# Self-attention and the masked cross-attention behind it in one block of a two-layer decoder kernel

## The reference

```python
x = _layernorm(x + _L0_attn_ref(x, ...))                  # gated recurrence
x = _layernorm(x + _L0_xattn_ref(x, ctx, ctx, mask, side, ...))
x = _layernorm(x + _L0_ffn_ref(x, ...))
x = _layernorm(x + _L1_attn_ref(x, ...))                  # self-attention, relative positions
x = _layernorm(x + _L1_xattn_ref(ctx, ctx, x, mask, ...)) # masked cross-attention
x = _layernorm(x + _L1_ffn_ref(x, ...))                   # gated feed-forward

# _L1_xattn_ref
k = (key @ Wk.T + bk); v = (value @ Wv.T + bv); q = (query @ Wq.T + bq)   # 16 heads each
scores = jnp.where(mask, q . k, -1e10)
out = softmax(scores / 4) . v
return out @ Wo.T + bo
```

## Time and profile before

| | us |
|---|---|
| median of 3 runs | 926.36 |
| lowest and highest | 924.04, 928.03 |
| profiled execution, its own time | 927.1 |
| its span in the trace | 925.3 |
| TensorE busy | 861.7 (93%) |
| VectorE busy | 681.9 (74%) |
| ScalarE busy | 620.9 (67%) |
| GpSimd busy | 413.0 (45%) |
| first and second barrier | at 298.0 and 627.7 |

### The profile page before, as it was taken

One profiled execution on the slowest core, in us unless ns is written; L12 is line 12 of the kernel. 1 busy time (PEld: TensorE's weight loads), 2 busy tenths in 40 slices (PEclk: granted clock), 3 DMA queues, 4 the chain that ended last, 5 costly groups with the idle time before them and its releaser, 6 DMA issues. The chain is left out here.

```text
span 925.3 us, 21117 instructions
## 1 busy us (share of the span) xinstructions
PE 861.7 (93%) x7006; PEld 621.4 (67%) x7017; DVE 681.9 (74%) x2515; ACT 620.9 (67%) x1608; POOL 413.0 (45%) x428
## 2 busy tenths in 40 slices
PE   9998989999987788999999999897999999999996
PEld 7876766777666466777777776675666666655554
DVE  4988888888877656687686676525888878866875
ACT  4548677777762367787787787735888888864441
POOL 2256246567342345434444342243455555326432
PEclk9999999999998899999999999997999999999998
DMA  9334100000005187797787788440000000000001
GB/s 327 115 113 117 42 24 24 25 24 13 13 25 204 55 279 241 226 277 219 244 251 227 242 256 253 140 165 4 27 27 28 27 28 24 2 2 1 24 24 46
DMA packets 96960, 101.89 MB, mean 110 GB/s; under 512 B 26877, under 2 KB 92157, under 8 KB 96598
## 3 DMA queue, kind: packets, MB, share of 16 engines
q1 hardware_dynamic: 96292, 100.20, 34.6%
q10 hardware_dynamic: 562, 0.35, 0.1%
HBM read 48.70 MB, written 51.82 MB: 109 GB/s over the span
## 5 line engine op out<-in xcount | busy, mean ns | idle before, releaser
L222 PE MATMUL bank<-x_feat,w_all_mats 128*128 128x256 f32 x384 | 94.6, 391 | 2.1 <-ACT q_full L340 0.6
L2746 POOL TENSOR_TENSOR bnd<-bnd,consts 128x60 f32<-128x60 f32 x64 | 18.1, 303 | 149.5 <-DMA bnd<-band_scratch 149.5
L222 PEld LDWEIGHTS bank<-x_feat,w_all_mats 128*128 128x128 f32 x384 | 71.0, 192 | 15.4 <-ACT rw L2404 4.3
L2364 ACT ACTIVATE bias_area<-bias_area,mq_two 128x256 f32<-128x256 f32 x128 | 66.2, 529 | 0.0
L1680 DVE COPY q_heads<-bank 128x512 f32<-128x512 f32 x64 | 42.7, 686 | 28.8 <-PE bank L1386 28.8
L1427 PE MATMUL bank<-dist,rw 128*128 128x512 bf16 x277 | 62.9, 379 | 0.7 <-issue 0.2
L845 ACT ACTIVATE q_heads<-bank 128x512 f32<-128x512 f32 x64 | 37.7, 589 | 37.9 <-PE bank L664 37.9
L2537 DVE COPY q_heads<-bank 128x512 f32<-128x512 f32 x64 | 41.4, 683 | 26.2 <-PE bank L2036 26.2
L931 DVE COPY q_heads<-bank 128x512 f32<-128x512 f32 x64 | 41.8, 683 | 25.3 <-PE bank L664 25.3
L837 ACT ACTIVATE Sx<-Sx,mq 128x256 f32<-128x256 f32 x128 | 54.4, 499 | 5.7 <-DVE mq L923 5.6
L1672 DVE CUSTOM_DVE_ANT_0 Sx<-bank,bias_area 128x256 f32<-128x256 f32 x128 | 46.5, 419 | 14.3 <-PE bank L1372 13.9
(11 more groups left out here) (275 smaller groups left out, 2494.8 us busy)
## 6 DMA issues: line engine op xcount, KB each, us to landing
dist<-skew_scratch SPq DMA_DIRECT2D x64, 296.0 KB, 4.2
skew_scratch<-rw SPq DMA_DIRECT2D x32, 588.0 KB, 4.5
bnd<-band_scratch SPq DMA_DIRECT2D x64, 108.0 KB, 2.7
band_scratch<-bias_area SPq DMA_DIRECT2D x32, 162.0 KB, 2.7
band_scratch<-bias_area SPq DMA_DIRECT2D x32, 148.0 KB, 2.5
skew_scratch<-dist SPq DMA_DIRECT2D x4, 1024.0 KB, 8.5
context_values<-dist SPq DMA_DIRECT2D x8, 512.0 KB, 2.6
v_two<-context_values SPq DMA_DIRECT2D x8, 512.0 KB, 3.5
```

The lines of the kernel that those rows point to most:

```text
L222: last = pe.matmul(dst[:, m * S:(m + 1) * S], w[:, k, m * P:(m + 1) * P], rhs[:, k, :], start=(k == 0), stop=(k == FT - 1))
L2364: last = act.activation(rows_of(n, g)[:, t, :], rows_of(n, g)[:, t, :], ACT.Exp, bias=mq_two[:, n % 2, g, t:t + 1], scale=-1.0, accum_out= ...
```

## The change

`attention_mask` no longer opens a block of its own. It returns its streams as functions (`scores`, `mask_pe`, `mask_act`, `mask_dve`, `mask_pool`, `mask_sp`), and `attention_relative` calls each at the end of its own stream. The second clearing of semaphores and the second barrier are gone; the first clearing takes 30 more semaphores, those of the recurrence and the loads.

On TensorE the scores of unit 0 stand in self-attention's tail ahead of the output product of batch 7; the query product of batch 1 goes to bank 6 behind it. The key products 13, 14 and 15 (`KV_LATE`; batches 5, 6 and 7) leave the tail and stand in the rounds of units 0, 3 and 4, in bank 7. The transposes of `x_tok` of batch 7 go to the round of unit 1. The three products' bias steps go from ScalarE to VectorE (`keep_late`), behind the scans of units 1, 4 and 5. VectorE's statistics of batch 7 go behind the scans of unit 0, and ScalarE's copies of batch 1's query and of batch 7's features into units 0 and 2.

```diff
-        KV_EARLY = 9
+        KV_EARLY, KV_LATE = 9, 13
...
-            return bank[i % 4 if i < KV_EARLY else 4 + i % 2]
+            return bank[i % 4 if i < KV_EARLY else 4 + i % 2 if i < KV_LATE else 7]
...
+        def keep_late(dve, i):
+
+            dve.wait_ge(kv_mm, i + 1)
+            for m in range(FT):
+                last = dve.tensor_scalar(batch(c_feat, i - B)[:, m, :], context_bank(i)[:, m * S:(m + 1) * S],
+                                         col(f"x1_bk{m}"), None, ALU.add)
+            last.then_inc(kv_sb, 1)
...
+                if j == 0 and b >= KV_EARLY - B:
+                    pe.wait_ge(kv_sb, B + b + 1)
...
+                    if b == 0:
+                        pe.wait_ge(sa_y_steps, 4 * (B - 1) + 1)
+                        project_context(pe, KV_LATE)
+                    if b == 1:
+                        pe.wait_ge(kv_sb, KV_LATE + 2)
+                        project_context(pe, KV_LATE + 2)
...
+                    if b == 0:
+                        pe.wait_ge(kv_sb, KV_LATE + 1)
+                        pe.wait_ge(sa_kept, B)
+                        transpose_tiles(pe, m_bank, x_tok[:, B - 1, :, :], sa_xt_mm)
...
+                    if b == 0:
+                        pe.wait_ge(q_sb, 3)
+                        project_context(pe, KV_LATE + 1)
                         weigh(n - 1)
...
+                        if n == 0:
+                            x1_copy_q(act, 1, o_bank)
+                        if n == 2:
+                            act.wait_ge(sa_xt_mm, B)
+                            act.activation(batch(x_feat, B - 1), m_bank[:, :].rearrange("p (f t) -> p f t", f=FT),
+                                           ACT.Copy).then_inc(sa_xt_sb, 1)
...
+                        if n == 0:
+                            dve.wait_ge(sa_biased, B)
+                            dve.wait_ge(sa_kept, B - 1)
+                            norm_begin(dve, sa_y_steps, B - 1, sa_y_mm, B, m_bank, True)
+                        if n in (1, 4, 5):
+                            keep_late(dve, KV_LATE + (1, 4, 5).index(n))
...
                     project_context(pe, KV_EARLY + 3)
-                    pe.wait_ge(rt_sb, B)
-                    mix_heads(B - 1, 0)
-                    project_context(pe, KV_EARLY + 4)
-                    pe.wait_ge(normed, FT * (B - 1) + 1)
-                    mix_heads(B - 1, 1)
-                    project_context(pe, KV_EARLY + 5)
-                    pe.wait_ge(normed, FT * B)
-                    project_rows(pe, m_bank, aT, wo, y_mm)
                     pe.wait_ge(kept, B - 1)
                     transpose_tiles(pe, s_bank[3], x_tok[:, B - 2, :, :], xt_mm)
-                    x1_project_q(pe, 1, s_bank[1])
+                    pe.wait_ge(rt_sb, B)
+                    mix_heads(B - 1, 0)
                     pe.wait_ge(x1_bv_wide, 1)
...
-                    project_context(pe, KV_EARLY + 6)
-                    pe.wait_ge(kept, B)
+                    pe.wait_ge(normed, FT * (B - 1) + 1)
+                    mix_heads(B - 1, 1)
                     pe.wait_ge(xt_sb, B - 1)
-                    transpose_tiles(pe, s_bank[3], x_tok[:, B - 1, :, :], xt_mm)
+                    pe.wait_ge(x1_bias_sb, 1)
+                    x1_scores(pe, 0)
+                    pe.wait_ge(normed, FT * B)
+                    project_rows(pe, m_bank, aT, wo, y_mm)
+                    pe.wait_ge(bt_sb, NQ * B)
+                    x1_project_q(pe, 1, o_bank)
+                    mask_pe(pe)
...
-        sublayer(attention_bias)
-        sublayer(attention_relative)
-        attention_mask()
+        nc.clear_and_free_semaphores([gz_mm, gh_mm, gg_mm, gy_mm, gx_mm, g_tanh, g_za, g_gate, g_h, g_y, g_steps, g_stat,
+                                       g_rstd, g_xn, g_half, g_evac, g_kept, g_zz, g_hb, loaded_wz, loaded_wh, loaded_wg,
+                                       loaded_x1, loaded_x0, loaded_x, loaded_c, loaded_w, loaded_small, x0_prep, x0_bv_wide])
+        nc.all_engine_barrier()
+        attention_relative()
```

More of the change, by code:

```diff
@@ new lines, in scores @@
+            def scores(pe, n):
+                b, j = divmod(n, NQ)
+                if j == 0 and b >= KV_EARLY - B:
+                    pe.wait_ge(kv_sb, B + b + 1)
+                pe.wait_ge(q_split, FT * b + j % 2 + 1)
+                ge(pe, s_max, TT * 4 * n)
+                for t in range(TT):
+                    for g in range(4):
+                        r = slice(32 * g, 32 * (g + 1))
+                        last = pe.matmul(s_bank[g][:, t * S:(t + 1) * S],
+                                         q_par[r, b % 2, j % 2, j // 2, t * P:(t + 1) * P],
+                                         batch(c_feat, b)[r, j // 2, :], start=True, stop=True)
+                last.then_inc(s_mm, 1)
@@ L1908, in _ @@
[L1908 to L1923 removed]
+                        else:
+                            pe.wait_ge(sa_xt_sb, B)
@@ new lines, in mask_pe @@
+                pe.wait_ge(kv_sb, KV_LATE)
+                for b in range(B):
+                    first_round(b, NQ * b)
+                    second_round(b, NQ * b + 1)
+                    third_round(b, NQ * b + 2)
+                    fourth_round(b, NQ * b + 3)
+                weigh(NQ * B - 1)
+                gate_up(1)
+                pe.wait_ge(kept, B - 1)
+                pe.wait_ge(y_steps, 4 * (B - 2) + 1)
+                transpose_tiles(pe, m_bank, x_tok[:, B - 2, :, :], xt_mm)
@@ new lines, in mask_sp, with load_values @@
+            def mask_sp(sp):
+                def load_values(b):
+                    ge(sp, pv_mm, NQ * (b - 1))
+                    x1_load_values(sp, b)
+                for b in range(2, B):
+                    x1_load_mask(sp, b)
+                    load_values(b)
+                for t in range(B):
+                    sp.wait_ge(xn_ready, t + 1)
+                    sp.dma_start(out[t].rearrange("(t p) f -> p t f", p=P), xn_two[t % 2][:, :, :])\
+                        .then_inc(stored[t % 2], 16)
+                for i in range(2):
+                    sp.wait_ge(stored[i], 16 * (B // 2))
@@ L1925, in attention_relative @@
+            return scores, mask_pe, mask_act, mask_dve, mask_pool, mask_sp
         def attention_relative():
@@ L2722, in _ @@
                     scale(B - 1, 1)
[L2723 to L2726 removed]
+                    for u in range(2):
+                        dve.wait_ge(c_out[0][u], 32 * (NQ * B // 2))
+                    dve.wait_ge(t_mm, 4 * NQ * B)
+                    mask_dve(dve)
                 @block.gpsimd
```

952 lines of the change are left out of this document (454 added, 498 removed).

## The result

The changed kernel takes 915.56 us (median of 6 runs, 913.97 to 918.63). The kernel before, run again beside it, takes 923.56 (median of 6, 922.37 to 928.03). The ratio is 0.9902, with a 95% interval of 0.9877 to 0.9926: 8.0 us between the medians, 9 by the ratio, 1% faster. The median before was 926.36 over its first three runs; the three runs added here took 922.37 to 923.08, so the zero of the forecast was high.

The account below looks back on a forecast made before the run. TensorE, busy 861.7 of 925.3 us, was taken as the bound, losing time at the seam to barrier, empty pipeline, half clock and unabsorbed key products. 11.15 gained minus 0.5 for clears, from 926.36, gave 915.7 us; range 912.8 to 920.6.

Parts of the forecast that it names:

- The path up to unit 1: TensorE from the first head mixing at 610.96: spacings sum to 11.64 us, unit 1's scores at 622.6 instead of 633.38.
- the uncovered filling: Between the first score product's end and ready exponentials: TensorE would lose 1.6 us unless output and query products cover it.
- The rounds: Rounds 0 to 4 take the moved work in 29.0 us; a key product of 1.73 us costs 0.82 in rounds 3 and 4.
- round 0: Unit 0's scores to the next: 5.5 us through VectorE's scans, statistics and copies; TensorE's own work would allow 5.1.
- The seam's sum: Up to unit 6's scores: they come at 651.6 instead of 662.77, 11.15 us gained; nothing changes behind.
- The bias steps: On VectorE behind the scans of units 1, 4 and 5: 0.8 us each, nothing on the path.
- The semaphores: First barrier: one more drain and two more range clears on GpSimd cost 0.5 us, at most 0.9.
- The total: Whole kernel: 11.15 less 0.5 gives 10.65 us gained, from a median of 926.36 to 915.7.
- Rival A: Rounds 0, 3 and 4 do not absorb the key products: 3.2 us less gain, 918.9; chance 0.11.
- Rival B: In the new first rounds TensorE's clock falls to half despite the closed gap: 4.4 us, 920.1; chance 0.11.
- Rival C: Products sharing bank 7 wait in single file for its emptying: up to 19.2 us, 934.9, slower; chance 0.03.
- Rival D: At the seam another wait holds the first scores or scans; 7.9 of 10.65 us stay lost, 923.6; chance 0.04.

Follow-up runs that it names:

- scores_late: Changed kernel with unit 0's score product moved behind the output product and batch 1's query product; 919.86 us, ratio to the kernel before 0.9946.
- keys_in_tail: Changed kernel with key products 13, 14 and 15 back in self-attention's tail, their bias steps on ScalarE; 918.65 us, ratio to the kernel before 0.9928.
- pause_only: Changed kernel, same order, with one added TensorE wait for VectorE's batch 7 statistics ahead of unit 0's first transposes; 915.86 us, ratio to the kernel before 0.9898.
- bias_on_act: Changed kernel with the three bias steps moved from VectorE to ScalarE; 913.80 us, ratio to the kernel before 0.9873.
- before_clears: Kernel before with only the first clearing enlarged by 30 semaphores in two more ranges; 926.19 us, ratio to the kernel before 1.0020.
- after_again: Changed kernel, unchanged, profiled and timed once more; 915.57 us, ratio to the kernel before 0.9893.
- before_again: Kernel before, unchanged, profiled once more; 922.44 us in one run.

## Why the prediction was right

It forecast 915.7 us within 912.8 to 920.6, faster with a chance of 0.93, and 915.56 was measured.

- **The path up to unit 1.** Forecast 11.64 us from the end of product 12's place to unit 1's scores, by spacings from other places of the old trace; it took 622.28 - 610.51 = 11.77. The bias product came at 1.69 instead of 1.58. scores_late shows what the cover is worth: without it the seam is 5.9 us longer. The prediction had priced the uncovered filling at 1.6 and half clock apart; there they came together, with a wait of 0.62 for VectorE's `aT` that it had not named.
- **The rounds.** 5.5, 5.64, 5.96, 5.96, 5.96 forecast, 5.32, 5.63, 5.97, 5.85, 5.85 measured, 0.4 us less in all. The idea that a round takes a product at less than its length is shown by keys_in_tail: the three cost 0 + 0.71 + 0.71. The term that was mis-sized most is round 0, by 0.18; its mechanism stands. The prediction let VectorE's statistics lengthen it, not TensorE's product, and it takes 5.32 with the product and without. In pause_only, where the statistics are over before the round begins, it takes 5.14.
- **The seam's sum.** 11.15 forecast against the first profile, 11.42 measured; against the second profile of the kernel before it is 9.97, so 1.45 us of the forecast gain hang on which execution was profiled.
- **The bias steps.** Taken at 0.8 us and off the path. They take 0.87 (0.48 each, as the row below shows), nobody waits for them, and bias_on_act shows that even their engine doesn't matter.

```profile
L563 DVE TENSOR_SCALAR c_feat<-bank,cols x6: 475/478/481, 626.7 to 649.4; 128x256 f32<-128x256 f32 x6
its engine sat idle before it (us, times) until:
who waited for it (us, times):
```

- **The semaphores.** 0.5 us forecast, 0.51 in the trace, though for two clears and two drains where the prediction counted one drain. The timed 1.4 of before_clears leaves open whether more hangs on it.
- **The total.** 10.65 us were forecast. The medians differ by 8.0 here and by 9.2 in after_again, and the ratios say 9 to 10. The forecast time was met nevertheless, since its zero, 926.36, was some 2 us above the other medians of before (923.97 to 924.89 on four chips). So hitting the time to 0.1 us is partly luck: a gain too large from a zero too high. A likely part of it, not shown for the timed runs, is that the gain was read against one profile whose seam had 10.2 us of half clock, where before_again had 6.8; before_clears had 10.2 again. The other candidate is the first barrier, above.
- **Rival A** (products not absorbed) is excluded by the rounds. **Rival B** (the clock falls) did not occur in any of the profiles with this order: the changed kernel twice, bias_on_act and pause_only twice. But scores_late shows how near it is: with the score product behind the two others it did. The prediction's reading against B, that the clock "fell only behind the gaps of 1.9 and 1.6 us", is wrong twice. The first stretch begins at 629.7, when the 1.6 us gap has not begun. And the second, from 640.0, comes behind these two shorter waits:

```profile
637.95 0.66 PE L1386 MATMUL bank<-ident,Sx 128*128 128x128 f32 x4 [1.04 <-ACT Sx L1574]
639.32 0.73 PE L1386 MATMUL bank<-ident,Sx 128*128 128x128 f32 x4 [0.71 <-ACT q_heads L1582]
```

  The same pair is followed by 3.4 us of half clock in before_clears and by none in before_again. So the argument that kept B at 0.11 was weaker than it looked, though B did not come true.
- **Rival C**, bank 7 in single file: no matmul into bank 7 waits in the seam. **Rival D**, another wait in place of the barrier: none.
- The rule of the Trainium skill that gave B its chance (TensorE: Matmul & The Clock Gate, "A second HAM failure mode: psum-queue depth-cycling") is not borne out here for the pauses of 0.7 to 0.9 us a round in the steady rounds, which stand at 1.00 in every profile. For the pair of 1.04 and 0.71 us just behind a stretch of half clock this case doesn't decide.

What was argued and not shown: what decides on the clock behind a pause. pause_only and scores_late differ in the pause's length, 1.45 and 1.73 us, in the work ahead of and behind it, and in the wait of 0.62 us that only scores_late has ahead of it. No run changed one alone. The same traces hold a nearer comparison in self-attention, where TensorE waits for the same step of VectorE ahead of the same score product. The rows are of before_again, before and bias_on_act:

```profile
578.60 1.15 PE L2022 MATMUL bank<-k_two,q_par 32*128 32x256 f32 x16 [1.40 <-DVE mq_two L2529]
580.30 1.15 PE L2022 MATMUL bank<-k_two,q_par 32*128 32x256 f32 x16 [2.04 <-DVE mq_two L2529]
579.01 1.15 PE L2064 MATMUL bank<-k_two,q_par 32*128 32x256 f32 x16 [2.18 <-DVE mq_two L2566]
```

In six of the 13 profiles this pause was 1.40 us, and the clock stayed at 1.00. In seven it was 2.04 to 2.28 us: 3.4 us of half clock begin near its end or up to 1.8 us behind it in six of them, and none in bias_on_act, at 2.18. So the longer pause goes with half clock here too, but its length alone does not settle it.

## What to carry to other kernels

At a seam between two stages, count three things apart: the barrier, the filling of the next pipeline, and the clock that falls behind the pauses. Here the barrier alone was worth 1 us of 10 to 11; what paid was to start the next stage's first step early enough that the old stage's last products cover its filling (5.9 us, half clock included). Then look in the next stage's steady rounds for free time of the bounding engine, and put there the work that has no urgent reader (4 us here): it costs its length minus that free time, and nothing where the round is bound by another engine's chain. To judge such a change, compare the distance between two landmarks of the trace, and the clock between them. In the three profiles of the changed seam it repeated to 0.01 us while their times spread by 5.9. Where the clock falls in it, as in the kernel before, it takes more than one profile: there it differed by 1.45.

## What the runs showed of the hardware

- After a pause of 1.73 us (scores_late) TensorE's granted clock was 0.50 for 6.8 us, in two of two profiles; after one of 1.45 us (pause_only) it stayed at 1.00, in two of two. In self-attention a pause of 2.18 us left it at 1.00 once, where 2.04 to 2.28 us went with 3.4 us of half clock six times. Pauses of 0.7 to 0.9 us in steady rounds never lowered it; 1.04 and 0.71 us, close behind a stretch of half clock, were followed by another in two of three profiles of the old order. In half clock the 16 matmuls of a score product took 2.09 us against 1.15.
- Clearing 30 more semaphores in two more ranges made TensorE wait 0.51 us longer at a barrier. On GpSimd, in the changed kernel, the added clears and drains were:

```profile
L2975 POOLq DRAIN  x2: 64/74/83, 298.5 to 298.7; - x2
L2975 POOLq EVENT_SEMAPHORE_RANGE_CLEAR  x2: 64/119/174, 298.6 to 298.8; - x2
```
